# All outputs of the values in one block, and the last pair's logits and scores at another place

## What is computed

```python
q = x @ w_q ; k = x @ w_k                                  # 8 heads of 64
gates = sigmoid(x @ w_gate)                                # per head, 8 experts
gm = one_hot(argmax(gates)) * gates
values = einsum('bhne,ehdk,bnd->bhnk', gm, value_experts, x)
sim = where(causal_mask, -big, einsum('bhid,bhjd->bhij', q * SCALE, k))
attn = softmax(sim)
out = einsum('bhij,bhjk->bhik', attn, values)
out = einsum('bhne,ehkd,bhnk->bhnd', gm, output_experts, out).sum(heads)
```

## Time and profile before

| | |
|---|---|
| median of 3 runs | 757.44 us (756.54 to 757.70) |
| the profiled execution's own time | 754.58 us |
| its span, first to last instruction | 752.8 us |
| PE busy | 733.5 us (97%) |
| DVE, ACT, POOL busy | 549.3, 381.3, 189.3 us |
| longest lines on PE | L1767 (values) 121.3 us, L1847 (products) 125.2 us, L1907 58.9 us |

### The profile page before, as it was taken

How to read it: one execution, slowest core, us unless ns; L and a number is a source line. 1 busy time by engine, 2 the same in 40 slices (tenths; PEclk the granted TensorE clock), 3 DMA queues, 4 the chain that set the end, 5 groups by cost and what they waited for, 6 DMA issues and landing times.

```text
span 752.8 us, 16813 instructions
## 1 busy us (share of the span) xinstructions
PE 733.5 (97%) x6551; PEld 556.0 (74%) x6551; DVE 549.3 (73%) x1642; ACT 381.3 (51%) x1063; POOL 189.3 (25%) x235
## 2 busy tenths in 40 slices
PE   7899999999999999999999999999999899999996
PEld 6666757775886578658866876688478778999996
DVE  4877785968777887788777876787959664265997
ACT  3755656346545554565456545643561446554422
POOL 0232521154015401540253025304210422000000
PEclk9999999999999999999999999999999999999999
DMA  7950020402040204020302130213204304000000
GB/s 230 397 125 1 29 57 2 112 1 58 5 111 2 57 14 101 2 56 24 92 1 57 34 81 11 48 42 73 57 2 114 113 13 102 1 1 1 15 22 22
DMA packets 56343, 43.07 MB, mean 57 GB/s; under 512 B 38541, under 2 KB 49445, under 8 KB 54857
## 3 DMA queue, kind: packets, MB, share of 16 engines
q1 hardware_dynamic: 56264, 42.01, 21.0%
HBM read 32.42 MB, written 9.58 MB: 56 GB/s over the span
## 4 chain that ended last, share of the span: by engine, by line
PE 87%; DVE 9%; issue 1%; ACT 1%; POOL 1%; DMA 0%; SPq 0%; DVEq 0%; ACTq 0%
PE ps L1767 15%; PE ps L1847 14%; PE ps L1907 8%; PE ps L2072 4%; PE ps L2050 4%; PE ps L1753 4%; PE ps L2019 4%; PE ps L1775 4%; PE ps L1859 3%; PE ps L1801 3%; PE ps L1788 3%; DVE shared L1494 2%; DVE shared L1487 2%; PE ps L1715 2%; PE ps L1930 2%; PE ps L1688 2%
## 5 line engine op out<-in xcount | busy, mean ns | idle before, releaser
L1767 PE MATMUL ps<-veF,hB 128*128 128x512 f32 x256 | 121.3, 606 | 0.0
L1313 DVE COPY_PREDICATED shared<-ghot,ps 128x512 f32<-128x512 int32 x128 | 88.0, 726 | 3.3 <-PE ps L1767 0.5
L859 ACT ACTIVATE sc<-sc,nmax 128x128 f32<-128x128 f32 (+1 forms) x128 | 57.2, 447 | 58.8 <-DVE nmax L1299 58.8
L1767 PEld LDWEIGHTS ps<-veF,hB 128*128 128x128 f32 x256 | 45.2, 189 | 51.3 <-issue 39.9
L659 POOL TENSOR_TENSOR sc<-sc,rg 128x384 f32<-128x384 f32 x64 | 51.6, 828 | 69.6 <-DVE rg L1286 69.6
L716 POOL TENSOR_TENSOR ve<-mv,eps 128x2 f32<-128x2 f32 x24 | 8.6, 357 | 235.5 <-DVE mv L1199 235.5
L1847 PE MATMUL ps<-early_masks,oeF 128*128 128x256 f32 x256 | 62.9, 385 | 0.0
L1847 PE MATMUL ps<-wide,oeF 128*128 128x256 f32 x256 | 62.3, 386 | 0.0
L2050 PE MATMUL ps<-hE,veF 128*128 128x256 f32 x256 | 59.5, 382 | 0.3 <-ACT wide L969 0.3
L1907 PE MATMUL ps<-hC,early 128*64 128x128 f32 x1024 | 58.9, 274 | 0.2
L1907 PEld LDWEIGHTS ps<-hC,early 128*64 128x64 f32 x1024 | 55.8, 137 | 2.5 <-issue 1.5
(11 more groups left out here) (253 smaller groups left out, 1520.3 us busy)
## 6 DMA issues: line engine op xcount, KB each, us to landing
chosen<-hot_scratch SPq DMA_DIRECT2D x16, 512.0 KB, 5.8
v_scratch<-shared SPq DMA_DIRECT2D x16, 512.0 KB, 5.0
vg<-v_scratch SPq DMA_DIRECT2D x16, 512.0 KB, 5.5
veF<-in_L_ffn_value_experts SPq DMA_DIRECT2D x1, 2048.0 KB, 10.0
oeF<-in_L_ffn_output_experts SPq DMA_DIRECT2D x1, 2048.0 KB, 15.5
early<-in_L_attn_w_qkv SPq DMA_DIRECT2D x1, 1536.0 KB, 16.0
shared<-bias_scratch SPq DMA_DIRECT2D x2, 512.0 KB, 4.7
veF<-in_L_ffn_W SPq DMA_DIRECT2D x1, 1024.0 KB, 5.4
```

Source lines behind the costliest of these rows:

```text
L859: act.activation(v, v, ACT.Exp, bias=nmax[:, h % RING, t:t + 1], scale=-1.0, accum_out=denB[:, h * T + t:h * T + t + 1]).then_inc(s_("f_e" ...
L1313: dve.copy_predicated(val[:, t, :].rearrange("p (h k) -> p h k", h=HF), ghot[:, t * HF:(t + 1) * HF, e].bitcast(I32).unsqueeze(2) .broadca ...
L1767: pe.matmul(ps[:, vbank(j), :], tok(hB, t), veF[:, :].rearrange("p (h e k) -> p e h k", h=HF, e=EF)[:, e, :, :], start=True, stop=True).th ...
```

## The change

On PE `logits(3)` moves from ahead of the values of `e` = 6 to behind those of `e` = 5, ahead of `turn_head(2)` and `turn_head(3)`. The tail becomes: the place "filled", the wait for all value copies, the place "turns", `turn_head(6)`, `turn_head(7)`, and then `outputs(0)` to `outputs(3)`.

On DVE the scores of head 7 are taken at `e` = 6, behind those of head 6, and `weights(3)` is taken at `e` = 7, ahead of the last two value copies.

On ACT `turned(0)` and `turned(1)` stand ahead of the exponentials of heads 4 and 6 and no longer behind them, and the copy of the first two outputs stands ahead of the place "turns". POOL's list is unchanged.

```diff
@@ ACT, values
                 for e in range(EF):
                     h = e
+                    if e >= 4 and e % 2 == 0:
+                        turned(e // 2 - 2)
                     for t in range(T):
...
-                    if e >= 4 and e % 2 == 0:
-                        turned(e // 2 - 2)
                     beside(e)
                 turned(2)
                 turned(3)
-                beside("turns")
                 act.wait_ge(s_("f_o"), b * 4 + 2)
                 act.activation(oT[:, 0:2, :], ps[:, 3, :], ACT.Copy).then_inc(s_("f_ots"), 1)
+                beside("turns")
                 beside("end")
@@ DVE, values
-                for e in range(EF):
-                    h = e
+                def scores(h):
                     for t in range(T):
...
+                for e in range(EF):
+                    if e < EF - 1:
+                        scores(e)
+                    if e == EF - 2:
+                        scores(EF - 1)
                     if e % 2 == 0 and e >= 2:
                         weights(e // 2 - 1)
+                    if e == EF - 1:
+                        weights(HF // 2 - 1)
                     for t in range(T):
                         waits = [(s_("f_v"), b * 16 + 2 * e + t + 1)]
...
                     beside(e)
-                weights(HF // 2 - 1)
                 beside("filled")
@@ PE, values
-                        if e % 2 == 0:
+                        if e in (2, 4):
                             pe.wait_ge(s_("f_sc"), b * 16 + 2 * e)
                             logits(e // 2)
                         value(2 * e)
...
+                    if e == 5:
+                        pe.wait_ge(s_("f_sc"), b * 16 + 12)
+                        logits(3)
                     if e >= 3 and e % 2 == 1:
                         turn_head(e - 3)
                         turn_head(e - 2)
...
                 pe.wait_ge(s_("f_vm"), b * 16 + 16)
-                for p in range(3):
-                    outputs(p)
+                beside("turns")
                 turn_head(6)
                 turn_head(7)
-                beside("turns")
-                outputs(3)
+                for p in range(4):
+                    outputs(p)
```

## The result

The changed kernel takes 765.47 us (median, 764.24 to 767.14) against 757.21 us for the kernel before, measured again beside it. The two medians lie 8.3 us apart; the ratio is 1.0117, with a 95% interval of 1.0106 to 1.0129, which is 8.9 us slower (8.0 to 9.8). The forecast was 764.9 us in a range of 760.3 to 768.3.

The account below looks back on a forecast made before the run. PE's order and its waits were taken to bound the kernel. Six stages at +1.2 us, batch 1 at +0.8 and batch 0 at -0.5 sum to +7.5 on 757.44, giving 764.9 us, range 760.3 to 768.3.

Parts of the forecast that it names:

- PE sets the end, and nothing behind gives back: Values stages: PE's order and waits set the end, so PE's loss there is lost outright; PE idles 19 us overall.
- The block saves 0.30 us a stage: PE's tail: one block of outputs in place of two saves 0.15 us twice, taking the tail from 5.61 to 5.31.
- The exponentials of head 7 are late: ACT, batch 3: head 7 done at 259.74, 0.2 us later; DVE's weights(3) waits for it, making value copies 1.5 us late.
- PE stands about 1.3 us: PE's tail, batch 3: after turned heads and turn1(., 1) at 260.37, PE stands until 261.65 to 261.8 for the value copies.
- PE behind a wait: PE's tail after the value copies: turn1(., 0) follows the wait at 0.44 us, ending at 262.15.
- turn1(., 3) and its cover: PE's tail: cover for DVE's copy of turn 1 falls to 0.44 us; timely copies would still leave 0 to 0.1.
- turn1(., 2) for ACT: Behind the output block: PE waits 0 to 0.2 us, taken as 0.1, for ACT's copy of turn1(., 0).
- Batches 0 and 1: First two stages: batch 1 +0.8 us (0.4 to 1.3), batch 0 -0.5 us (0 to -0.8).
- Rival 1: All eight stages: one block pays 0.30 us each and head 7's exponentials bind nothing, giving 754.4 us, faster; 8%.

Follow-up runs that it names:

- one_more_block: Kernel before with turn_head(6) placed between outputs(1) and outputs(2), giving three blocks of outputs per values stage: 758.93 us, ratio 1.0034.
- turned_behind_6: Changed kernel with ACT's turned heads 0 to 3 put back behind the exponentials of heads 4 and 6: 766.86 us, ratio 1.0137.
- turn_first: Changed kernel with PE's turn of the normed tokens (MODULATE, place 5) moved ahead of logits(3) and the heads 2 and 3: 757.83 us, ratio 1.0016.
- weights_back: Changed kernel with DVE's weights(3) put back behind the last two value copies: 760.55 us, ratio 1.0062.
- block_only: Kernel before with only PE's new tail (turns, heads 6 and 7, then all four outputs): 762.27 us, ratio 1.0075.
- turned_behind_7: Changed kernel with ACT's turned(1) moved behind the exponentials of head 7: 761.57 us, ratio 1.0068.

## Why the prediction was right

**PE sets the end, and nothing behind gives back.** Right. The tail lengths of the three kinds of stages add up to the measured difference, and PE's busy time did not change (733.5 and 733.3 us). I had expected 2.4 us less of it; that was wrong, for the reason under "PE behind a wait". The forecast time lies 0.6 us from the measured median, which is closer than the sum of the changes was (7.5 us for 8.8). That is luck: the medians lie 0.6 us nearer to each other than the ratio has it, and the kernel before read 0.2 us lower than in the forecast.

**The block saves 0.30 us a stage.** Right in the changed kernel (32 outputs in 2.75 us, six heads in 0.66), and right by itself (one_more_block, 0.32). The rule that a change of the tiling mode drains the array ("TensorEngine Tiling (Array Packing)", section Key Properties, in the Trainium skill) agrees with that; the price is the trace's.

**The exponentials of head 7 are late.** Right, and the numbers held: from the end of PE's turn to the end of head 7 I had 4.09 us, and the chain has 258.02 to 262.05, 4.03. DVE stands 1.6 us at L1282 at the longest, eight times, as forecast. The copies end 5.75 us after PE's turn, where I had 5.95. Only the reason that I gave for it was partly off. I wrote that `turned(1)` "used to fill the time in which ACT waited for head 7's scores, and now stands in front"; turned_behind_6 shows that the edit that put it in front of head 6 does nothing. It stood ahead of head 7 before too. What changed is that ACT starts this list 1.0 us later and that the value copies now hang on its end. turn_first takes away the first, weights_back the second, and each gives back much of the loss. `hV` starts 1.92 us behind the end of value 11 (256.13 to 258.05) for 0.92 before (253.91 to 254.83); 0.86 of it are `logits(3)`, as forecast. The other 0.14 are the heads 2 and 3, which take 0.80 behind the logits and 0.66 before; I had them at 0.66 in any order. PE itself lost nothing by that: the eight values behind take 3.63 us behind the logits and 3.44 behind the turn (weights_back).

**PE stands about 1.3 us.** Right: 7.7 us in six stages, 1.3 in batch 1, 0.4 in batch 0.

**PE behind a wait.** Mis-sized. I gave PE 0.05 to 0.2 us of hand-over behind the value copies and took the work that follows at its length in a closed row, one without a wait in it. The four transposes behind a wait take 0.63 to 0.66 us in the chain where the same four take 0.44 behind other work, about 0.2 us more, and the changed stage has two such pieces ahead of the heads and one behind the outputs (0.63 for 0.59). That is also why PE's busy time did not fall by the 2.4 us of the blocks.

**turn1(., 3) and its cover.** I wrote that with timely copies the shorter cover "would leave 0 to 0.1". It leaves 0.4 (block_only, turned_behind_7, weights_back: 2.4 to 2.6 us in six stages). Turn 1 itself ends at 260.37, so that DVE's 0.69 us can't be done before 261.06 however early the value copies are, and turn 3 was due at 260.81. In the changed kernel the chain gives this wait 0.01 us, but the starts show that it is longer. In a closed row turn 3 would start 0.44 behind turn 0, at 264.26; it starts at 264.48. DVE's timeline has the copy at

```profile
263.66 0.67 DVE L1427 COPY prT<-ps 128x512 f32<-128x512 f32 x1
```

so it ends at 264.33, and turn 3 starts 0.15 behind it, which is the hand-over that the chains of block_only and turn_first show from this copy (0.14). The place costs 0.2 us; I had priced it at 0.12 (262.15 to 262.27).

**turn1(., 2) for ACT.** Right: 0.15 us between the outputs' end (268.50) and 268.65, for which I had taken 0.1 in 0 to 0.2.

**Batches 0 and 1.** -0.33 and +0.85 for -0.5 and +0.8. Per stage of the other six it was +1.39 for +1.2, so that the sum was 8.8 for 7.5; the 0.2 us are the restarts.

**Rival 1, faster by the block.** It was to decide at head 7's exponentials being done by about 258.6, counted in the before stage's time. turn_first reaches just that (`weights(3)` begins at 258.62, value 11 ending at 253.91 in both), and is at 1.0016, not at 0.996: the point where the wait ends was right, but the price at that point left out the wait of turn 3, which with its restart is worth 0.33 us a stage there (tail 12.08 against 11.75). With turn 3 moved as well, the time is under that of before, by 0.8 us and not by 3, and that from batches 0 and 1.

## What to carry to other kernels

When work is pulled forward on one engine, ask whether its consumer's in-order list can start sooner; here the scores of head 7 came over 2 us earlier, but ACT's list ahead of them began with copies whose producer had been pushed back by the very instructions pulled forward. A small step (0.22 us) that feeds a busy engine belongs ahead of the step that feeds it later. And joining two short blocks takes cover away from whatever lay between them: price what the pieces in the middle were hiding (here a copy on DVE and the weighing on POOL) before counting the change of mode that is saved.

## What was not expected of the hardware

A wait of PE costs more than the wait that the profile shows. In the timeline of the changed kernel a single 128x128 transpose lasts 0.27 us at the median, while four of them in a closed row take 0.44, 0.11 each: they overlap by 0.16. The profile models the ends of matmuls and counts a wait from there; from start to start a wait costs the overlap as well, and turn 3 above shows that in its starts alone (0.66 behind turn 0, where a closed row has 0.44). A wait breaks the overlap. The four transposes behind one take 0.63 to 0.66 us, whether the wait before them is 1.3 us (changed) or 0.4 (block_only), and at the full granted clock (0.999 over the changed kernel). So in these stages a place where PE stands costs some 0.2 us on top, two thirds of what a whole block of outputs costs to enter and leave, and a wait shown as 0.01 us cost that much. The median stands in the profile of line L1950:

```profile
L1950 PE MATMUL ps<-ident,wide x128: 272/273/332, 186.2 to 646.2; 128*128 128x128 f32 x128
```
